# Masks before scores: the order of TensorE's matmuls in a causal attention's row-score units

## What is computed

```
h = concat([patches(x) @ W_embed + b + pos, txt], axis=1)        # 64 x 228 x 256
q, k, v = heads(layernorm(h) @ Wq.T), ...                        # 16 heads of 16
scores = einsum('bhqd,bhkd->bhqk', q, k) / sqrt(16)
scores = where(triu(ones, k=1), -inf, scores)
probs  = softmax(scores)
h = h + (probs @ v) @ Wo.T + bo
h = h + ternary_linear(gelu(ternary_linear(layernorm(h), w_up)), w_down)
```

## Time and profile before

| | |
|---|---|
| median of 3 runs | 2037.98 us (2035.65 to 2040.5) |
| the profiled execution's own time | 2038.7 us |
| its span, first to last instruction | 2037.0 us |
| mean granted TensorE clock | 0.981 |
| busy: PE, PEld | 1927.0 us (95%), 1570.8 us (77%) |
| busy: DVE, ACT, POOL | 1467.2 us (72%), 1312.1 us (64%), 893.7 us (44%) |

### The profile page before, as it was taken

One profiled execution on the slowest core, in us unless ns is written; L12 is line 12 of the kernel. 1 busy time (PEld: TensorE's weight loads), 2 busy tenths in 40 slices (PEclk: granted clock), 3 DMA queues, 4 the chain that ended last, 5 costly groups with the idle time before them and its releaser, 6 DMA issues.

```text
span 2037.0 us, 59822 instructions
## 1 busy us (share of the span) xinstructions
PE 1927.0 (95%) x25090; PEld 1570.8 (77%) x25090; DVE 1467.2 (72%) x2717; ACT 1312.1 (64%) x1986; POOL 893.7 (44%) x1067
## 2 busy tenths in 40 slices
PE   4789999999999999999999999999999999999875
PEld 3668878778878877777877877887787788788654
DVE  3667778777777777777777777787777777777753
ACT  3447666666776666766666677666677666767652
POOL 1124444544444444444454444444444445444443
PEclk8889999999999999999999999999999999999987
DMA  5011111111111101111111111110111111010000
GB/s 147 15 45 40 55 50 51 44 35 45 50 50 55 50 28 51 40 54 50 52 44 33 45 50 50 55 50 29 50 42 53 50 54 50 25 50 21 30 29 23
DMA packets 66117, 93.72 MB, mean 46 GB/s; under 512 B 10083, under 2 KB 59719, under 8 KB 65593
## 3 DMA queue, kind: packets, MB, share of 16 engines
q1 hardware_dynamic: 65848, 89.90, 15.6%
HBM read 45.03 MB, written 14.94 MB: 29 GB/s over the span
## 4 chain that ended last, share of the span: by engine, by line
PE 89%; DVE 5%; ACT 2%; issue 2%; POOL 1%; DMA 1%; SPq 0%; ACTq 0%; DVEq 0%; POOLq 0%
PE dense L324 50%; PE score L324 21%; PE pvps L324 9%; PE dense L342 4%; PE dense L381 2%; DVE aT_lo L896 2%; PE dense L544 2%; PE dense L370 1%; POOL acc L1168 1%; ACT aT_hi L655 1%; DVE mx L946 1%; DMA borow<-bo 1%; ACT pr L668 0%; DVE mx L945 0%; DVE st L930 0%
## 5 line engine op out<-in xcount | busy, mean ns | idle before, releaser
L1149 POOL TENSOR_SCALAR_AFFINE_SELECT pr<-pr 114x456 f32<-114x456 f32 x512 | 311.7, 633 | 868.2 <-ACT pr L668 868.1
L668 ACT ACTIVATE pr<-score 114x1368 f32<-114x1368 f32 x256 | 335.7, 1311 | 296.5 <-PE score L324 296.1
L945 DVE TENSOR_REDUCE mx<-score 114x4 f32<-114x456 f32 x256 | 161.4, 630 | 261.9 <-PE score L324 261.5
L946 DVE TENSOR_REDUCE mx<-score 114x4 f32<-114x912 f32 x256 | 281.4, 1099 | 0.0
L324 PE MATMUL dense<-wdn,g 128*114 128x256 bf16 x1024 | 241.7, 281 | 2.0 <-ACT g L677 1.2
L324 PE MATMUL score<-qm,km 32*114 32x228 f32 (+1 forms) x4096 | 221.3, 330 | 18.8 <-DVE mx L946 15.6
L324 PE MATMUL dense<-wdn,gl 128*114 128x256 bf16 x1024 | 234.8, 275 | 0.0
L1168 POOL TENSOR_TENSOR acc<-acc,sq 128x456 f32<-128x456 f32 x192 | 222.5, 1159 | 18.9 <-POOL acc L1168 0.4
L324 PEld LDWEIGHTS score<-qm,km 32*114 32x114 f32 x4096 | 175.6, 174 | 69.5 <-issue 40.3
L324 PE MATMUL score<-km,qm 32*114 32x114 f32 (+1 forms) x4096 | 222.1, 331 | 7.4 <-ACT pr L668 6.7
L324 PE MATMUL pvps<-pr,vp 114*32 114x228 f32 (+1 forms) x4096 | 205.2, 318 | 0.7 <-POOL pr L1149 0.4
(11 more groups left out here) (125 smaller groups left out, 4432.2 us busy)
## 6 DMA issues: line engine op xcount, KB each, us to landing
pix<-x SPq DMA_DIRECT2D x64, 588.0 KB
rs<-raw SPq DMA_DIRECT2D x256, 57.0 KB, 2.0
cx<-raw SPq DMA_DIRECT2D x256, 57.0 KB, 2.0
out<-h SPq DMA_DIRECT2D x64, 228.0 KB
h<-txt SPq DMA_DIRECT2D x32, 64.0 KB, 7.2
km<-wqkvo SPq DMA_DIRECT2D x1, 1024.0 KB, 13.6
h<-w_upT SPq DMA_DIRECT2D x1, 1024.0 KB, 13.9
km<-w_embed SPq DMA_DIRECT2D x1, 768.0 KB, 6.6
```

The costliest lines, as they stand in the source:

```text
L668: act(pr[q % 2][:], score[0:R, :, 0:SW], ACT.Exp, scale=float(HD) ** -0.5).then_inc(a["exp"], 1)
L945: nc.vector.tensor_reduce(mx[:, m, 0, x:128:32], score[0:R, :, 0:R], AX.X, ALU.max)
L946: nc.vector.tensor_reduce(mx[:, m, 1, x:128:32], score[0:R, :, R:SW], AX.X, ALU.max).then_inc(v["max"], 1)
L1149: nc.gpsimd.affine_select(out=blocks, in_=blocks, compare_op=ALU.is_ge, fill=0.0, base=0, pattern=[[0, 4], [1, R]], channel_multiplier=-1) ...
```

## The change

In `scores_rows`, the 16 mask matmuls come ahead of the 8 score matmuls. The first mask shape (j = 0, the widest) opens the accumulation in each bank, the other masks and then the scores are added; the columns that no mask covers are written by the scores first. The last score matmul closes the group and carries the semaphore. The wait for `score_emptied` now stands first, and in steps 0 to 3 the waits for queries and keys stand between the masks and the scores. Nothing else differs.

```
@@ -488,25 +488,25 @@
 
                 b, r = divmod(k, 4)
                 m, par = divmod(r, 2)
+                eng.wait_ge(*score_emptied(t, k, False))
+                for j in range(4):
+                    for i in range(4):
+                        o = score[0:R, i, 0:SW].rearrange("p (x w) -> p x w", w=R)[:, 0:3:2, 32 * j:R]
+                        above = cmask[quad(i), 96:96 + R - 32 * j].rearrange("p (o w) -> p o w", o=1)
+                        mm(o, idm[quad(i), 96 - 32 * j:96 - 32 * j + R], above.broadcast_to([32, 2, R - 32 * j]),
+                           start=(j == 0), stop=False, skip_group_check=True)
                 if b == 0:
                     eng.wait_ge(a["q"], count(4, t - 1, 2 * m + par + 1))
                     if par == 0:
                         eng.wait_ge(v["km"], count(2, t - 1, m + 1))
                     else:
                         eng.wait_ge(a["km"], count(2, t - 1, m + 1))
-
-                eng.wait_ge(*score_emptied(t, k, False))
                 for qb in range(2):
                     for i in range(4):
-                        mm(score[0:R, i, qb * R:qb * S + R], qm[quad(i), par, 1 - u, m, b * S + qb * R:b * S + qb * R + R],
-                           km[quad(i), 1 - u, m, par, b * S:b * S + R + qb * R], start=True, stop=False,
-                           skip_group_check=True)
-                for j in range(4):
-                    for i in range(4):
-                        o = score[0:R, i, 0:SW].rearrange("p (x w) -> p x w", w=R)[:, 0:3:2, 32 * j:R]
-                        above = cmask[quad(i), 96:96 + R - 32 * j].rearrange("p (o w) -> p o w", o=1)
-                        last = mm(o, idm[quad(i), 96 - 32 * j:96 - 32 * j + R], above.broadcast_to([32, 2, R - 32 * j]),
-                                  start=False, stop=True, skip_group_check=True)
+                        last = mm(score[0:R, i, qb * R:qb * S + R],
+                                  qm[quad(i), par, 1 - u, m, b * S + qb * R:b * S + qb * R + R],
+                                  km[quad(i), 1 - u, m, par, b * S:b * S + R + qb * R], start=False, stop=True,
+                                  skip_group_check=True)
                 last.then_inc(pe["s"], 1)
```

## The result

The changed kernel took 2046.43 us (median of 6 runs, 2045.09 to 2046.99), the kernel before 2039.64 us (median of 6, the three of the table above among them). The ratio is 1.0037 with a 95% interval of 1.0026 to 1.0047: slower by 6.8 us by the medians, 7.5 by the ratio, with bounds of 5.3 and 9.6 us. The profiled execution of the change took 2045.09 us; its span is 2043.4 us, 6.4 us longer than before.

The account below looks back on a forecast made before the run. TensorE, busy 95% of the span, was taken as the bound. Per row-score unit -0.05 + 0.10 - 0.02 = +0.03 us, times 226 units, gave +6.8 us on the median 2037.98: 2044.8 us, range 2038 to 2050.

Parts of the forecast that it names:

- Entry, -0.05 us: At the row-score unit's start, the unhidden first load becomes bf16 (0.05) instead of float32 (0.10): -0.05 us a unit.
- The bare float32 load, +0.10, less 0.02: Between masks and scores, a float32 load stands unhidden, +0.10 us; the last mask's 0.02 us stream now lies under it.
- The exit stays, and VectorE's release with it: At the unit's end, the 0.11 us to the next stage's load stays, and the column-score unit awaiting VectorE's maxima sees no change.
- 226 units of 256: Step 7's units stand before the aT_lo wait, which absorbs their growth; 226 units at +0.03 us remain: +6.8 us.
- the start and the end: Units outside 300 to 1840 us: dearer at the 1.2 GHz level, free in front of waits; taken to cancel.
- The moved waits at nothing: In steps 0 to 3, query and key waits moved behind the masks gain nothing and were costed at nothing.
- the rival that gave them 3.8 us: The moved waits cost 0.03 us in each of 128 units of steps 0 to 3: +3.8, 2048.6 us; chance 9%.
- No change that can be told: Rival: bare score load half covered, +0.01 us a unit, 2040.3 us, or more units stand before waits; chance 17%.
- The load pulled ahead: Rival: the scores' float32 load runs beside the mask groups, -0.05 us a unit, -11.3 us, 2026.7 us; chance 9%.
- The emptied array: Rival: going from bf16 to float32 empties the array, +0.12 us a unit, +27 us, 2065 us; chance 5%.
- The rule that speaks otherwise: Skill's rule: load time is columns / 1.2 ns whatever the type; +0.08 us a unit, 18 us, 2056 us; chance 2%.

Follow-up runs that it names:

- (1): Changed kernel with the masks run from the narrowest (36 columns) to the widest (228): 2035.41 us, ratio 0.9975 against the kernel before.
- (2): Kernel before with only the widest mask moved ahead of the scores, the other three staying behind them: 2025.57 us, ratio 0.9928 against the kernel before.
- (4): Kernel before, scores still first, with only the masks reversed, narrowest to widest: 2046.63 us, ratio 1.0030 against the kernel before.
- (5): Changed kernel with the masks' stationary operand at 128 columns in place of 114: 2037.96 us, ratio 0.9990 against the kernel before.
- experiment 3: Changed kernel with the waits for queries and keys put ahead of the masks again: 2047.61 us, ratio 1.0036 against the kernel before.
- experiment 6: Kernel before reordered to widest mask, scores, other masks, with a 128-column mask operand: 2021.06 us, ratio 0.9904 against the kernel before.

## Why the prediction was right, point by point

The forecast was 2044.8 us, +6.8 on a median of 2037.98. Measured were 2046.43 and +6.8 on a median of 2039.64: the kernel before has a median 1.7 us higher with more runs, and the difference of the two is the forecast's. That it agrees to 0.1 us is luck, as the terms below show; that the sign and size agree is not.

**Entry, -0.05 us.** Right. After the change the second mask group starts 0.15 after the unit's load: 0.05 until the next load begins, and 0.10 of stream.

**The bare float32 load, +0.10, less 0.02.** Right. In the change the second score load begins 0.10 after the first. Four experiments bear it out: hide the load behind a wide mask and the unit falls to 1.01 (1) or 0.97 (2); leave the scores first and make a stream short ahead of a load, and the same 0.03 to 0.04 appear (4); shorten the mask's load alone and the masks-first unit falls to 1.01 (5). The unit rose from 1.02 to 1.05, in nanoseconds from 1.024 to 1.050, in each of steps 0 to 6: +0.026 where 0.03 was forecast.

**The exit stays, and VectorE's release with it.** Half right. The unit's own exit stayed (after the change the last score group starts 0.76 behind the unit's load and streams 0.19, and the next stage's load comes at 1.05, 0.10 later), but the maxima start later behind a float32 end. In step 5 the next stage's load, the maxima and the load of the column unit that waits for them stand at 1039.40, 1039.52 and 1041.29 before (the earlier trace rows for the last):

```profile
1039.40 0.13 PEld L324 LDWEIGHTS dense<-wdn,g 128*114 128x114 bf16 x1
...
1039.52 0.64 DVE L945 TENSOR_REDUCE mx<-score 114x4 f32<-114x456 f32 x1
1040.07 1.10 DVE L946 TENSOR_REDUCE mx<-score 114x4 f32<-114x912 f32 x1
```

After the change, the stage behind the unit, its last matmul, the column load, and the maxima:

```profile
1041.76 0.32 PE L324 MATMUL dense<-wdn,g 128*114 128x256 bf16 x1
...
1043.45 0.27 PE L324 MATMUL dense<-wdn,gl 128*114 128x256 bf16 x1
...
1043.68 0.17 PEld L324 LDWEIGHTS score<-qm,km 32*114 32x114 f32 x1 [0.20 <-issue]
...
1041.91 0.63 DVE L945 TENSOR_REDUCE mx<-score 114x4 f32<-114x456 f32 x1
1042.46 1.10 DVE L946 TENSOR_REDUCE mx<-score 114x4 f32<-114x912 f32 x1
```

They begin 0.15 after the stage's load in place of 0.12, and the column load comes 0.23 after the last dense matmul in place of 0.20. The second of the maxima ends 0.12 ahead of the column load in both (1041.17 to 1041.29, 1043.56 to 1043.68), so the load follows them. In experiment 4, where a mask ends the unit, both are back, 0.11 and 0.21:

```profile
1042.63 0.32 PE L324 MATMUL dense<-wdn,g 128*114 128x256 bf16 x1
...
1042.74 0.63 DVE L945 TENSOR_REDUCE mx<-score 114x4 f32<-114x456 f32 x1
...
1044.31 0.27 PE L324 MATMUL dense<-wdn,gl 128*114 128x256 bf16 x1
...
1044.52 0.17 PEld L324 LDWEIGHTS score<-qm,km 32*114 32x114 f32 x1 [0.18 <-issue]
```

So the change has a second, small cost of about 0.02 us in each iteration's step 5, which the prediction had at nothing. The transposes of step 6 also start later: 0.20 behind the last down matmul in place of the 0.17 before (1050.37 to 1050.54). In the table both delays stand in all four kernels whose unit ends with a float32 score, and are smaller or absent in the four where it ends with a mask. By which way the delay reaches the transposes is argued, not shown. Before, then after:

```profile
1050.54 0.97 PE L381 MATMUL dense<-ident,xn 114*128 114x114 f32 x8
```

```profile
1052.78 0.27 PE L324 MATMUL dense<-wdn,gl 128*114 128x256 bf16 x1
1052.98 0.97 PE L381 MATMUL dense<-ident,xn 114*128 114x114 f32 x8
```

**226 units of 256.** Right in kind: the aT_lo wait fell from 15.2 to 14.5 us over 26 times, 0.03 each, and took the growth of step 7's units. What the units, steps 5 and 6 make together is seen over six whole iterations, from one step-0 unit to that six later. Before, then after:

```profile
339.17 0.35 PE L324 MATMUL score<-km,qm 32*114 32x114 f32 x2
...
698.76 0.35 PE L324 MATMUL score<-km,qm 32*114 32x114 f32 x2
```

```profile
339.40 0.31 PE L324 MATMUL score<-cmask,idm 32*114 32x228 bf16 x3
...
700.60 0.31 PE L324 MATMUL score<-cmask,idm 32*114 32x228 bf16 x3
```

359.59 us against 361.20: 0.27 us an iteration. In nanoseconds, seven units at 0.026 are 0.18, steps 5 and 6 another 0.05, and 0.04 lies in shifts of about 0.01 us each in steps 0, 1, 2 and 7, whose cause is not shown. Over 32 iterations 0.27 would be 8.6 us, more than the 6.8 measured. In the profiled executions the 29 iterations from the third on grew by 6.0 us and not by 7.8: two of them are longer in the kernel before, which had 1.0 us of "issue" gaps there that the changed one lacks, and come out 0.6 and 0.3 us shorter after the change. All that stands ahead of and behind these 29 grew by 0.4 us: 0.6 less until the first unit, 0.1 more in the first two iterations, 0.9 more at the end. So the start and the end did not quite cancel, as I had let them. The forecast had the unit too dear (226 x 0.026 would be 5.9 us), had 0.09 us an iteration at nothing, and knew of no gaps; that these errors of opposite sign left 6.8 is chance.

**The moved waits at nothing.** Right to within 0.03 us an iteration (experiment 3), and the rival that gave them 3.8 us falls. **No change that can be told:** falls. The interval of the ratio excludes it, and the score load is not half covered: its 0.10 us stands bare. **The load pulled ahead:** falls. In the score units of all eight profiles no load begins before the last matmul ahead of it in its own row group has begun, and so never two ahead. **The emptied array:** falls by experiments 1 and 2.

**The rule that speaks otherwise.** The load at 114 columns is not as long as in float32; the mask group spacing after the change (0.15 with the entry) says 0.05, so the 2056 us that the rule gave did not come. At 128 columns a bf16 load gets shorter still: in experiment 6 the next load follows after 0.02 us. The Trainium skill, TensorE: Matmul & The Clock Gate (Weight-path perf modes), has a faster load for 128 columns that are not float32, and the trace agrees. That it works in row groups of 32 too is what experiments 5 and 6 show.

## What to carry to other kernels

Where TensorE is the bound, count not only streams but bare weight loads. In these traces each load hides behind the one matmul before it, so what costs is a long load behind a short stream, and the first load after the array has been regrouped. Order a mixed sequence so that the unit opens with its shortest load and the widest cheap stream stands ahead of the longest load. Here that was worth 0.29 us of an iteration of 59.93 (about 9 us of 2040; the 15 measured hold more clock as well), and 0.51 with a 128-column operand, while the same matmuls in the wrong order cost 0.27. To price a unit, compare whole iterations in the steady part of the run: the run's time also holds its start, its end and the clock that is granted there.

## What had not been expected of the hardware

A 128-column bf16 operand, 14 columns of it useless, loads faster than one of 114: the next load follows after 0.02 us instead of 0.05, also in row groups of 32 (experiments 2 and 6). And VectorE's maxima start later, counted from TensorE's next stage, when the last matmul ahead of them is a 228-column float32 one: 0.15 us behind that stage's load, against 0.12 behind a 36-column bf16 mask and 0.11 behind a 228-column bf16 mask (experiment 4). So it is not the width that delays them.
